# Attention and routed experts in one kernel: keys of two heads in one weight block, contexts written inside the first steps, maxima two units later in the first half

## The reference, cut to what matters

```python
xn = _layernorm(x)                            # x: (32, 256, 128)
ctx = xn @ We.T                               # 16 columns
influence = ctx @ ctx.T                       # per batch, 256 x 256
Q, K, V = heads(Wq), heads(Wk), heads(Wv)     # 16 heads of 8
scores = (Q @ K.T) * SCALE + 0.1 * influence[:, None]
attn = softmax(scores);  out = (attn @ V) @ Wo.T
# beside it: 8 experts, the best 2 for each row, gelu(xn @ w1 + b1) @ w2 + b2,
# weighted with their probabilities
x = x + attention(xn) + experts(xn)
```

## Time and profile before

| | us |
|---|---|
| median of 3 runs | 710.17 |
| lowest, highest | 706.68, 710.49 |
| the profiled execution, its own time | 709.09 |
| its span, first to last instruction | 707.3 |
| TensorE, VectorE, ScalarE, GpSimd busy | 648.5, 614.3, 541.5, 467.4 |

### The profile page before, as it was taken

One profiled execution on the slowest core, in us unless ns is written; L12 is line 12 of the kernel. 1 busy time (PEld: TensorE's weight loads), 2 busy tenths in 40 slices (PEclk: granted clock), 3 DMA queues, 4 the chain that ended last, 5 costly groups with the idle time before them and its releaser, 6 DMA issues.

```text
span 707.3 us, 24553 instructions
## 1 busy us (share of the span) xinstructions
PE 648.5 (92%) x7800; PEld 433.7 (61%) x7800; DVE 614.3 (87%) x1106; ACT 541.5 (77%) x1123; POOL 467.4 (66%) x542
## 2 busy tenths in 40 slices
PE   0377899999999999989999999999999999999996
PEld 0264345555555555579999999998455555555553
DVE  8989789899999999868888888888999999999991
ACT  2592378888888888788888888888778877878775
POOL 8680468676687757135565565565687888778774
PEclk9986799999999999999999999999999999999999
DMA  8859556766766766684554454452667788787742
GB/s 244 318 161 331 151 146 167 203 180 171 194 171 183 202 172 175 155 132 93 107 107 94 106 101 106 100 107 70 148 165 186 179 185 183 175 185 186 178 112 79
DMA packets 162948, 113.32 MB, mean 160 GB/s; under 512 B 72625, under 2 KB 150449, under 8 KB 162865
## 3 DMA queue, kind: packets, MB, share of 16 engines
q1 hardware_dynamic: 153632, 90.63, 52.5%
q0 software_dynamic: 8192, 16.86, 9.7%
q10 hardware_dynamic: 1040, 4.76, 1.8%
HBM read 55.42 MB, written 47.19 MB: 145 GB/s over the span
## 4 chain that ended last, share of the span: by engine, by line
PE 70%; DVE 12%; SPq 6%; DMA 4%; issue 4%; ACT 3%; ACTq 0%; DVEq 0%
PE bank L1133 14%; PE bank L1251 14%; PE bank L1111 13%; PE mx L1240 13%; PE mx L1145 8%; DVE mx L955 5%; DMA stack<-qk_dram 3%; PE bank L1031 3%; PE bank L1193 2%; DVE A L790 2%; PE bank L1155 1%; PE bank L1162 1%; ACT A L707 1%; SPq L318 1%; DMA stack<-mT 1%
## 5 line engine op out<-in xcount | busy, mean ns | idle before, releaser
L707 ACT ACTIVATE A<-bank 128x512 f32<-128x512 f32 x502 | 278.3, 597 | 63.6 <-PE bank L1133 55.9
L955 DVE TENSOR_REDUCE mx<-mx 128x4 f16<-128x1024 f32 x256 | 302.6, 1205 | 20.0 <-PE mx L1145 14.5
L578 POOL TENSOR_SCALAR rows<-rows,slot_p 128x128 f32<-128x128 f32 x142 | 112.0, 798 | 95.8 <-DVE rows L1008 95.8
L1133 PE MATMUL bank<-stack 113*128 113x256 f16 x1004 | 170.7, 277 | 1.7 <-ACT A L707 0.8
L564 POOL DMA_INDIRECT slots_x<-rows,pos x128 | 123.6, 966 | 52.9 <-PE bank L1133 34.0
L608 POOL DMA_INDIRECT rows<-slots_y,pos x128 | 121.3, 948 | 40.8 <-PE bank L1133 19.7
L1111 PE MATMUL bank<-A,V 128*32 128x256 f32 x2048 | 137.3, 386 | 1.7 <-ACT A L707 1.6
L751 ACT ACTIVATE rows<-mx,b 128x256 f32<-128x256 f32 x284 | 111.5, 474 | 25.7 <-PE mx L1240 23.9
L1133 PEld LDWEIGHTS bank<-stack 113*128 113x128 f16 x1004 | 72.9, 98 | 89.4 <-ACT A L707 56.4
L1000 DVE TENSOR_TENSOR rows<-rows 128x512 f16<-128x512 f32 x142 | 101.1, 713 | 25.1 <-ACT rows L755 22.6
L1251 PE MATMUL bank<-w,rows 128*128 x1704 | 107.3, 219 | 1.3 <-DVE rows L1000 1.3
(11 more groups left out here) (142 smaller groups left out, 596.2 us busy)
## 6 DMA issues: line engine op xcount, KB each, us to landing
stack<-ctx_rest SPq DMA_DIRECT2D x64, 256.0 KB
stack<-qk_dram SPq DMA_DIRECT2D x128, 96.0 KB
slots_y<-rows SPq DMA_DIRECT2D x71, 128.0 KB, 2.0
qk_dram<-hi_qk SPq DMA_DIRECT2D x64, 128.0 KB
stack<-ctx_high SPq DMA_DIRECT2D x128, 64.0 KB
slots_x<-A ACTq DMA_DIRECT2D x1, 4644.0 KB, 19.8
w_stage<-in_w SPq DMA_DIRECT2D x8, 512.0 KB
qk_dram<-lo_qk SPq DMA_DIRECT2D x64, 64.0 KB
```

Of the source, the lines that this page charges most:

```text
L578: ins = pool.tensor_scalar(ye[n % 4][:, h, :], ye[n % 4][:, h, :], slot_p[:, n // 4 % 3, n % 4, h:h + 1], None, ALU.mult)
L707: act.activation(A[:, n % NA, :, :].rearrange("p h s -> p (h s)"), scores(k, n)[:, :], ACT.Exp, scale=SCALE).then_inc(s_xp, 1)
L955: dve.tensor_reduce(mx[:, a, 8 * qt:8 * qt + 8].rearrange("q (i e w) -> q i e w", i=2, e=2)[:, :, g % 2], MX[u % 2][:, :].rearrange("q (i ...
L1133: mm = pe.matmul(scores(k, n)[:, i * S:(i + 1) * S], stack[0:SHIFT + 1, par, h, 1, c * P:(c + 1) * P], stack[0:SHIFT + 1, par, h, 0, :], s ...
```

## The change

1. Keys of two heads share a block. `stack` is now `[P, 2, 6, 4, S]`: blocks 0 to 3 hold the queries of four heads each, blocks 4 and 5 the keys of eight heads, in four places. Two heads of different classes have their keys in one place, in their own rows. `shifted` makes their scores with one weight load and one product of 512 columns. `plain` takes its operands from the new places. A load of half a stack is six DMAs (the shared context rows of queries and keys apart), 512 KB where it was 576 KB, counted by `s_st` to 96; the layout of `qk_dram` and `ctx_high` follows, so that one DMA of the write has 256 pieces of 512 bytes instead of 128 of 1 KB, and each write of `ctx_high` has twice the bytes. The start values of `stack` shrink with it.
2. Contexts 1 to 3 are written at the end of steps -1, 0 and 1. `part_c` has a tile of its own, and the exponentials don't wait for it. Both halves of the clears are issued by ScalarE's queue, the second after three normalised groups.
3. In the first half the maxima are made two units later (`LAG = 2`): units 2 to 7 make `v` of 0 to 5 of batch `k+1`, units 0 and 1 of the next step `v` of 6 and 7. SP issues the `SHIFT` rows of heads 8 to 15 first in a step, and those of heads 0 to 7 behind the write of the projections. The second half keeps its order.
4. `START` is 8.

```diff
-START = 4
+START = 8
+LAG = 2
...
+def maxima_of(u, s, f, first_half):
+    v = (u - LAG) % 8 if first_half else u
+    off = 0 if v > u else 1
+    return v, f["m" if off else "n"], s.at(off)
...
-        stack = sb("stack", [P, 2, H, 2, S], F16)
+        stack = sb("stack", [P, 2, 6, 4, S], F16)
+        part_c = sb("part_c", [P, 4, 2, 2 * S], F16)
...
             def load(half2, par2, g):
...
-                rest = rest.rearrange("o c (n t) -> (o c n) t", n=2).unsqueeze(1).to_broadcast([2 * DE, 8, 2 * S])
-                sp.dma_start(stack[REST:REST + 2 * DE, par2, 8 * g:8 * g + 8, :, :], rest).then_inc(s_st[par2][g], 16)
+                rest = rest.rearrange("o c (n t) -> (o c n) t", n=2).unsqueeze(1)
+                dst = stack[REST:REST + 2 * DE, par2, 2 * g:2 * g + 2, :, :].rearrange("r b w t -> r (b w) t")
+                sp.dma_start(dst, rest[:, :, 0:S].to_broadcast([2 * DE, 8, S])).then_inc(s_st[par2][g], 16)
+                sp.dma_start(stack[REST:REST + 2 * DE, par2, 4 + g, :, :], rest[:, :, S:2 * S].to_broadcast([2 * DE, 4, S])).then_inc(s_st[par2][g], 16)
...
             write(0, 1, 1)
-            clear(sp, 8, 10)
             context(0)
             sp.wait_ge(s_cw[0], 96)
             for g in range(2):
                 load(0, 0, g)
             write(1, 2, 2)
-            clear(sp, 10, 14)
-            context(1)
-            clear(sp, 14, 16)
-            context(2)
-            context(3)
...
-                if k == 1:
-                    for r in range(1, 4):
-                        sp.wait_ge(s_cw[r], 96)
+                if first_half and f["n"]:
+                    shift_rows(1, b, par)
                 for g in range(2):
...
                     if f["l"]:
                         if k is None or k >= 0:
                             sp.wait_ge(s_ex, 16 * b + 8 * g + 8)
                         load(half2, par2, g)
-                    if f["m"]:
+                    if f["m"] and not first_half:
                         shift_rows(g, b1_, par1)
                     if g == 0 and f["p"]:
...
                         write(par3, n_hq, n_lq)
+                    if g == 0 and f["m"] and first_half:
+                        shift_rows(0, b1_, par1)
+                if k in (-1, 0, 1):
+                    context(k + 2)
+                if k == 1:
+                    for r in range(1, 4):
+                        sp.wait_ge(s_cw[r], 96)
...
             for g in range(3):
                 normalise(g)
+            clear(act, 8, 16)
...
-                classes = stack[:, par].rearrange("r (a i h) s t -> r i a h s t", a=2, i=2)
+                classes = stack[:, par, 0:4].rearrange("r (a i) h t -> r i a (h t)", i=2)
                 dve.memset(classes[0:64, 1], 0.0)
-                ins = dve.memset(classes[64:P, 0, :, :, 0], 0.0)
+                ins = dve.memset(classes[64:P, 0], 0.0)
...
-                        for i in range(2):
-                            h = 8 * (g // 2) + 4 * p + 2 * (g % 2) + i
-                            mm = pe.matmul(scores(k, n)[:, i * S:(i + 1) * S], stack[0:SHIFT + 1, par, h, 1, c * P:(c + 1) * P], stack[0:SHIFT + 1, par, h, 0, :], start=True, stop=True)
-                        mm.then_inc(s_ex, 1)
+                        h, w = 8 * (g // 2), 2 * (g % 2) + p
+                        pe.matmul(scores(k, n)[:, :], k_side(par, h + w)[0:SHIFT + 1, c * P:(c + 1) * P], stack[0:SHIFT + 1, par, h // 4:h // 4 + 2, w, :], start=True, stop=True).then_inc(s_ex, 1)
...
-                    if f["m"] and u % 2 == 0:
-                        for v in (u, u + 1):
-                            plain(v)
+                    v, wanted, of = maxima_of(u, s, f, phase[0] == 0)
+                    if wanted and u % 2 == 0:
+                        plain(v, *of)
+                        plain(v + 1, *of)
```

More of the change, by code:

```diff
@@ L83, in attention_flags @@
     first, last = (0, HALF - 1) if b0 == 0 else (b0, B - 1)
-    ahead = {"p": 3, "l": 2, "m": 1}
+    ahead = {"p": 3, "l": 2, "m": 1, "n": 1}
     return {s: first + (ahead.get(s, 0) if b0 else 0) <= k + off <= last + (0 if b0 else ahead.get(s, 0))
-            for s, off in (("p", 3), ("l", 2), ("m", 1), ("x", 0), ("o", -1), ("c", -2))}
-ALL = dict.fromkeys("plmxoc", True)
+            for s, off in (("p", 3), ("l", 2), ("m", 1), ("n", 0), ("x", 0), ("o", -1), ("c", -2))}
+ALL = dict.fromkeys("plmnxoc", True)
+def maxima_of(u, s, f, first_half):
+    v = (u - LAG) % 8 if first_half else u
+    off = 0 if v > u else 1
+    return v, f["m" if off else "n"], s.at(off)
 def attention_steps(eng, b0, body):
@@ L192, in build @@
         zeros = A[:, 1:NA // 2, :, :].rearrange("p n h s -> p (n h s)")[:, 0:ZROWS * RW // 2]
-        part_c = [A[:, NA // 2 + r, :, :].rearrange("p h s -> p (h s)").bitcast(F16).rearrange("p (a t) -> p a t", a=2) for r in range(4)]
         early = w12[:, :, :].rearrange("p a n -> p (a n)")
@@ L240, in scores, with q_side, k_side, both_sides @@
             return ring[n % len(ring)] if k == B - 1 else EX[n % 2]
+        def q_side(par, h):
+            return stack[:, par, h // 4, h % 4, :]
+        def k_side(par, h):
+            return stack[:, par, 4 + h // 8, h % 4, :]
+        def both_sides(row, n, par, g, i):
+            first_, second_ = 2 * g + i, 4 + g
+            return stack[row:row + n, par, first_:second_ + 1:second_ - first_, :, :]
         def head_values(par, c, g, i):
@@ L314, in context @@
                 for q in range(2):
-                    lo, hi = (part_c[r][:, a:a + 1, q * S:(q + 1) * S] for a in range(2))
+                    lo, hi = (part_c[:, r, a:a + 1, q * S:(q + 1) * S] for a in range(2))
                     high, rest = (c[q, 4 * r:4 * r + 4].rearrange("i c (m t) -> (i c) m t", t=S) for c in (ctx_high, ctx_rest))
-                    sp.dma_start(high, hi.to_broadcast([P, 2, S])).then_inc(s_cw[r], 16)
+                    sp.dma_start(high, hi.to_broadcast([P, 4, S])).then_inc(s_cw[r], 16)
                     sp.dma_start(rest[:, 1:3], hi.to_broadcast([P, 2, S])).then_inc(s_cw[r], 16)
@@ L362, in shift_rows @@
                 for c in range(2):
-                    sp.dma_start(stack[SHIFT:SHIFT + 1, par1, 8 * a:8 * a + 8, 0, c * P:(c + 1) * P], mT[8 * c:8 * c + 8, par1, a, :]).then_inc(s_mr[par1][a], 16)
+                    sp.dma_start(stack[SHIFT:SHIFT + 1, par1, 2 * a:2 * a + 2, :, c * P:(c + 1) * P].rearrange("r b w t -> r (b w) t"), mT[8 * c:8 * c + 8, par1, a, :]).then_inc(s_mr[par1][a], 16)
             xs = slots_x.bitcast(F16).rearrange("(n s) c -> n s c", s=SLOT)
@@ L486, in _ @@
             for par in range(2):
-                pool.memset(stack[64:P, par, :, 1, :], -1.0).then_inc(s_post, 1)
+                pool.memset(stack[64:P, par, 4:6, :, :], -1.0).then_inc(s_post, 1)
                 pool.wait_ge(s_post, par + 1)
@@ L552, in _ @@
             places(0, Tb)
-            pool.wait_ge(s_zero, 64)
+            pool.wait_ge(s_zero, 32)
             pool.wait_ge(s_prob, 1)
@@ L700, in attend @@
                             if k == 0 and n == 0:
-                                act.wait_ge(s_zero, 64)
+                                act.wait_ge(s_zero, 32)
                             if k != 0 or g >= 2:
                                 act.wait_ge(s_pv, 4 * b + g - 1)
-                            if k == 0 and n == NA // 2:
-                                for sm in s_cw:
-                                    act.wait_ge(sm, 96)
                             act.activation(A[:, n % NA, :, :].rearrange("p h s -> p (h s)"), scores(k, n)[:, :], ACT.Exp, scale=SCALE).then_inc(s_xp, 1)
@@ L977, in attend @@
                         dve.wait_ge(s_ot, bo + 1)
-                        v = MISC[:, :].rearrange("q (h r) -> q h r", r=16)
-                        dve.reciprocal(rden[:, :], v[:, :, DK]).then_inc(s_rd, 1)
+                        heads = MISC[:, :].rearrange("q (h r) -> q h r", r=16)
+                        dve.reciprocal(rden[:, :], heads[:, :, DK]).then_inc(s_rd, 1)
                         dve.wait_ge(s_rd, bo + 1 + c_rd)
```

60 lines of the change are left out of this document (30 added, 30 removed).

## The result

| | before | after |
|---|---|---|
| median of the runs, us | 710.33 (706.68 to 710.52, 4 runs) | 731.61 (730.60 to 733.08, 4 runs) |
| ratio | | 1.0309, 95% interval 1.0288 to 1.0331 |
| span of the profiled execution, us | 707.3 | 729.7 |

What follows compares the result with a forecast made beforehand. TensorE was taken to bound the steps, with VectorE close behind. The terms 11.0 + 0.5 - 1.2 - 1.3 - 0.5 + 0.5 = +9.0, on the median of 710.17, gave 719.2 us; range 702 to 733.

Steps and rivals of the forecast that it cites:

- start, up to step 1 (with the memset): Before the steps: VectorE's idle time and two reductions saved, -5.6 us; smaller memset of the stack's key side, -1.2.
- rows of heads 8 to 15, steps 1 and 2: Middle of steps 1 and 2: SHIFT rows arrive late behind a context on SP's queue, about 2 and 4 us, +6.1.
- ring, steps 4 to 15: Head, unit 3, load, write, rows of heads 0 to 7, next head: 14.3 us against a 13.38 step, +11.0.
- end of the first half: Two reductions and transposes (3.2 us) after the last exponentials, mostly beside other work: +0.5 us, up to +2.
- second half, shared weights, loads: One product of 512 columns for two of 256 in the second half, -1.3 us; smaller half-stack loads, -0.5.
- VectorE's route: From head through unit 4's products, reductions, transposes and row landing to the next head: at most 13.1 us, not deciding.
- The clears at 0: Clears on ScalarE's queue at the start: issue hidden in its waits for VectorE, zero, up to +2 without that cover.
- The weights' load ahead of the rows: Even steps: a 512 KB weight load queued ahead of the rows of heads 8 to 15; zero, bound +1 each, 6 times.
- Shared weights: Products of two heads sharing one weight load, already hidden: 0.005 us a pair, second half, -1.3, from 0 to -3.
- rival 4: Weight loads were not hidden: halving them takes 0.098 us a pair off 512 pairs, -50, 660 us; chance 0.03.
- Rivals 1 and 3: 1: start wins, ring doesn't bind, about -8, 702 us, chance 0.20. 3: it all cancels, 710 us, chance 0.15.
- Rival 2: Full queues: rows behind load and write land in 4.31 us, ring 16.5, +38; at 3.2, +24; heavier ring's chance 0.12.

Runs made afterwards that it cites:

- rows_first: The changed kernel with the SHIFT rows of heads 0 to 7 issued ahead of the write of the projections in the first half, lag kept: 740.63 us.
- rows_first_w: rows_first with the 512 KB load of the first layer's weights moved behind the rows of heads 8 to 15: 727.01 us.
- ring_only: lag_act with the changed kernel's own order of SP's queue, rows of heads 0 to 7 behind the write: 722.73 us.
- lag_act: Changed kernel with second clear on SP's queue, contexts 2 and 3 on ScalarE's, rows of heads 0 to 7 before the write, weights' load behind rows: 712.58 us.
- warm: The changed kernel with useless products meant in front of three of TensorE's waits; only the first filler, in step 1, took effect: 729.38 us.
- clear_back: The changed kernel with the second clear back on SP's queue, in two parts behind the two first writes: 731.73 us.
- clear_late: The changed kernel with the second clear issued 35 us later on ScalarE's queue, at 49.51 instead of 14.15: 733.17 us.
- no_lag_mid_sp: no_lag_mid with the 4.6 MB clear on SP's queue, as in clear_back: 713.84 us.
- no_lag_mid: no_lag with context 3 written behind context 2 in step 0 instead of in step 1: 718.23 us.
- ctx_front: The changed kernel with contexts 1 to 3 written in front of step -1 as before, lag kept, clears still on ScalarE's queue: 727.50 us.
- no_lag: The changed kernel with LAG = 0 and SP's old order of the SHIFT rows, everything else of the change kept: 718.60 us.

## Why the prediction was right or wrong

The direction and the main term were right; the size was not, 21.3 for 9.0. What failed is how the sum priced a wait, and the clears that it put at nothing. By the terms of the forecast, in us of the V projections' starts:

| term | forecast | measured |
|---|---|---|
| start, up to step 1 (with the memset) | -6.8 | -2.9 |
| rows of heads 8 to 15, steps 1 and 2 | +6.1 | +10.7 |
| ring, steps 4 to 15 | +11.0 | +12.1 |
| end of the first half | +0.5 | +2.2 |
| second half, shared weights, loads | -1.8 | +0.6 |
| sum | +9.0 | +22.7 |

Of the 13.7 us that the sum missed, 5.1 are slower products behind three waits, 2.5 the clear, 2.4 the second half, 1.7 the end of the first half, and 1.0 longer waits in steps 1 and 2. The rest is small. All but one small part err to the same side, so 731.6 is inside the range of 702 to 733 for reasons that the range was not made for.

**The ring** was right in place and cause, and nearly in size, with some luck. 14.3 us were worked out, 12.2 to the second row DMA and 2.1 to land; most steps take 14.2, 12.4 and 1.8 in the one from the head at 176.56 to that at 190.76, so 0.2 too little and 0.3 too much cancel. TensorE is idle for 0.6 at the head, and for 0.4 ahead of it for VectorE. The +12.1 are 8.9 in the eleven steps from 4 on, where 10.1 was forecast for as many, and 3.3 in the one before them, whose wait of 1.65 has 1.6 of slower products behind it. Taking the rows from behind the write removes the ring (rows_first, rows_first_w); putting it back costs 10.1 (ring_only against lag_act). Not all of the longer step is the ring: with the rows ahead of the write it still takes 13.5 to 13.7, where the kernel before has 13.2 and 13.6, so the "at most 13.1" for VectorE's route was a little low. A row DMA lands in 1.7 to 1.8 us in the ring, under the 2.1 taken. The Trainium skill gives 2.0 as a DMA's fixed part, for GpSimd's path (DMA: Bandwidth & Descriptors, Anatomy of one DMA); on SP's queue this case stays under it.

**The rows in steps 1 and 2: the step that failed most.** The waits were sized at 2 and 4 and are 2.85 and 4.25, with the mechanism as written, the landing of the last context in front of the second. But the sum took a wait at its own length. TensorE comes out of it at the lower clock: from the end of the wait to unit 6's unshifted products it is 4.01 and 4.51 us instead of the 2.52 in the run warm, or the 2.51 of the changed kernel's own step 3 (137.46 to 139.97), which has no such wait. 1.5 + 2.0 + 2.85 + 4.25 = 10.6, the measured 10.7. Warm shows this for the first; for the second, and for the 1.6 at the head of step 4, it is read from the rows, not tried. Nor does the length of a wait alone settle it: behind 1.71 us in clear_back the clock stayed, behind 1.11 in ring_only it did not.

**The clears at 0 ("up to +2 without that cover").** The cover named was the wrong one. The load of the first context is wanted late, but the write of the projections is not: its last DMA takes 10.10 us to land while the second clear of 4.6 MB is under way (issued at 14.15, landed 32.4 us later), ScalarE waits for that write before the next `hi_qk`, and VectorE behind it. With the clear elsewhere (clear_back, clear_late) ScalarE does not wait there. VectorE's wait is 4.92; up to step 1 it costs 2.5 (clear_back against the changed kernel). With clear_back's start the gain at step 1 is 5.4 of the 6.8 forecast. The memset's part of it came: the first write of the projections is issued at 32.40, where it was at 33.88. Yet the clear is not part of the 21.3 in the sense that taking it back would help: clear_back is not faster, because SP's queue decides steps 1 and 2. Without the lag it was worth 4.4 (no_lag_mid_sp against no_lag_mid, in the medians).

**The weights' load ahead of the rows**, "bound +1 a time", was bounded too low: up to 3.8 (17.28 against 13.52 in rows_first). In the changed kernel the ring covers it, as the prediction said, but for one step of 15.06 in which TensorE waits 0.56 for these rows behind such a load.

**The end of the first half** has two more units of maxima behind the last step. The experts' first product waits 0.66 for them, in the changed kernel and in lag_act, and comes 1.9 later after the last V projection than before. +2.2, where 0.5 was taken and 2 given as the bound.

**Shared weights** gained nothing: 13.19 to 13.21 a step in the second half, and 13.20 to 13.22 before; the +0.6 in the table is the last step alone (13.57 for 12.43). This bears out rows 8 against rival 4. The Trainium skill's rule behind that rival is that a weight load overlaps products only in another row group (TensorE: Matmul & The Clock Gate, Part 3; the same part also names a background buffer for weights, which no run here can show). The trace doesn't agree with that "only": these loads and products all span 113 rows, and without overlap one load less would have taken rival 4's 0.098 us off each of 16 pairs, 1.6 a step.

Rivals 1 and 3 did not come about; rival 1's gain at the start exists (5.4) but is given back two steps later. Rival 2, a row DMA at 4.3 behind a full queue, is not what the ring shows, but is what rows_first found with the weights' load ahead (4.5).

What stays open: 6.9 us for the lag in the repaired kernel, of which the profiled executions account for 4.3 (1.9 + 0.9 in the steps, 2.4 at the end of the half, less 0.9 at the start). Why the ring_only runs spread over 6.7 us was not tried either; the two long steps in its profile follow waits in the ring of 1.36 and 1.11, the second with slower products behind it. What decides whether the clock falls behind a wait is open too. `START` = 8, the load in six DMAs and the smaller memset stayed in every run and were not priced alone.

## What to carry to other kernels

A queue that issues small, urgent transfers is a resource with an order: for each step moved on it, list what is issued next and who waits for that, and put bulk loads behind the rows that gate the next product. Where a change makes TensorE wait, price the wait and the slower products that may follow it, here 1.5 to 2 us more behind waits of 1.65 to 4.25. Work that is taken out of a chain at the start should go to a queue that is idle then, not later into the same queue: on ScalarE's, 5.9 us idle twice, contexts 2 and 3 made the kernel 8.2 us faster than behind each other on SP's (713.84 to 705.68), while moving context 3 one step forward on SP's queue changed nothing (718.60 and 718.23).

## What the runs showed of the hardware

- Waits of TensorE of 1.62, 1.65, 1.83, 2.29, 2.39, 2.56, 2.85, 4.25 and 6.78 us were each followed by products at 1.2 GHz (ctx_front, the changed kernel, rows_first, warm, ctx_front, ring_only, the changed kernel twice, no_lag). Behind the 1.65, 2.85 and 4.25 this lost 1.6, 1.5 and 2.0 us. After waits of 1.10 (warm), 1.44 (ring_only), 1.59 (rows_first) and 1.71 (clear_back) the products ran at full speed. One of 1.11 (ring_only, at 209.33) was followed by sixteen products in 1.94 us instead of 1.07. So the length of the wait alone doesn't tell. With twelve products of 512 columns in place of the first 2.85 (warm) the clock stayed at 1.00.
- The landing of a row transfer of 2 KB, from the start of its issue: 1.7 to 1.8 us as a rule in the changed kernel's ring, 2.96 behind a context's six writes (the chain of the changed kernel at 99.79), 4.5 behind a load of 512 KB issued 1.2 us earlier on the same queue (rows_first).
- A 4.6 MB clear on ScalarE's queue delays a small write on SP's. With the clear under way the last DMA of the write took 10.10 us to land and ScalarE waited 4.48 for it; in clear_back and clear_late it did not wait there. In clear_late, with the clear issued at 49.51, it waited 7.74 us for a later write. In the changed kernel the two clears landed 20.5 and 32.4 us after their issue.
